# Rotary partners of queries and keys by an exchange of partition halves, with the sine products on GpSimd

## The reference, cut to what matters

```python
def rotate_half(x):
    x1 = x[..., ::2]
    x2 = x[..., 1::2]
    return jnp.stack((-x2, x1), axis=-1).reshape(x.shape)
q, k, v = (proj(Wq, bq), proj(Wk, bk), proj(Wv, bv))
q = q * cos + rotate_half(q) * sin
k = k * cos + rotate_half(k) * sin
attn = jnp.einsum('bhqd,bhkd->bhqk', q, k) * scale
attn = jax.nn.softmax(attn, axis=-1)
```

## Time and profile before

| | |
|---|---|
| median of 3 runs | 600.16 us (597.83 to 601.16) |
| the profiled execution | 598.14 us, span of the core 596.4 us |
| busy share of the span | PE 95%, DVE 83%, ACT 70%, POOL 65% |
| granted TensorE clock, mean | 0.997 |

### The profile page before, as it was taken

One profiled execution on the slowest core, in us unless ns is written; L12 is line 12 of the kernel. 1 busy time (PEld: TensorE's weight loads), 2 busy tenths in 40 slices (PEclk: granted clock), 3 DMA queues, 4 the chain that ended last, 5 costly groups with the idle time before them and its releaser, 6 DMA issues.

```text
span 596.4 us, 19146 instructions
## 1 busy us (share of the span) xinstructions
PE 568.1 (95%) x6702; PEld 438.2 (73%) x6702; DVE 495.8 (83%) x1445; ACT 415.0 (70%) x1038; POOL 385.3 (65%) x817
## 2 busy tenths in 40 slices
PE   8778999999999999999999998999999999999895
PEld 6555666777777777777677786788888888888774
DVE  3679889898988898987788888788888899889763
ACT  1104678778887777788888767767887777777652
POOL 4755556667776667677667776666666677764422
PEclk9989999999999999999999999999999999999999
DMA  7656666566766666745545644335544445441000
GB/s 220 178 157 146 164 155 152 131 151 156 175 152 154 150 150 150 176 117 140 134 117 126 156 128 103 90 90 128 118 119 120 130 128 129 115 121 36 12 20 23
DMA packets 74657, 76.25 MB, mean 128 GB/s; under 512 B 10348, under 2 KB 68908, under 8 KB 70092
## 3 DMA queue, kind: packets, MB, share of 16 engines
q1 hardware_dynamic: 63636, 68.09, 45.0%
q10 hardware_dynamic: 10920, 6.88, 5.5%
HBM read 46.86 MB, written 23.33 MB: 118 GB/s over the span
## 4 chain that ended last, share of the span: by engine, by line
PE 70%; DVE 19%; issue 4%; ACT 3%; POOL 3%; DMA 1%; SPq 0%; ACTq 0%; DVEq 0%; POOLq 0%
PE banks L1630 15%; PE banks L1571 10%; PE banks L1606 9%; PE banks L1472 7%; PE banks L1535 7%; DVE top L1156 5%; DVE top L1155 3%; PE banks L1524 3%; DVE neg_shift L1150 2%; PE banks L1525 2%; PE banks L1504 2%; PE banks L1574 2%; DVE top_sums L1177 1%; DVE top_sums L1180 1%; PE banks L1482 1%
## 5 line engine op out<-in xcount | busy, mean ns | idle before, releaser
L1366 ACT ACTIVATE probs_t<-banks 128x512 f32<-128x512 f32 (+1 forms) x496 | 259.2, 551 | 72.3 <-PE banks L1606 47.8
L1150 DVE TENSOR_REDUCE neg_shift<-banks 128x2 f32<-128x512 f32 x256 | 165.7, 681 | 31.5 <-PE banks L1571 30.0
L1630 PE MATMUL banks<-probs_t,v_ext 128*32 128x256 f32 (+1 forms) x2048 | 116.8, 357 | 0.0
L1571 PE MATMUL banks<-k_stack,q_stack 72*128 72x256 bf16 x512 | 99.7, 276 | 8.0 <-DVE neg_shift L1150 3.3
L1156 DVE MAX8 top<-banks 128x8 f32<-128x256 f32 x256 | 106.1, 414 | 0.0
L1606 PE MATMUL banks<-q_stack,k_stack 75*128 75x256 bf16 x512 | 98.4, 273 | 0.3 <-ACT probs_t L1366 0.2
L1155 DVE MAX8 top<-banks 128x8 f32<-128x128 f32 x256 | 74.1, 290 | 19.8 <-PE banks L1580 19.4
L1026 POOL TENSOR_TENSOR hidden<-up_tanh,gate_half 128x256 f32<-128x256 f32 x93 | 68.3, 736 | 28.6 <-DVE up_tanh L1209 23.5
L1630 PEld LDWEIGHTS banks<-probs_t,v_ext 128*32 128x32 f32 x2048 | 55.4, 109 | 38.8 <-issue 12.8
L1571 PEld LDWEIGHTS banks<-k_stack,q_stack 72*128 72x128 bf16 x512 | 40.4, 98 | 48.1 <-DVE neg_shift L1150 36.4
L1524 PE MATMUL banks<-f_xT_high,w_gate_up 128*128 128x256 f32 x192 | 57.5, 322 | 2.3 <-DVE up_tanh L1209 2.0
(11 more groups left out here) (123 smaller groups left out, 1366.9 us busy)
## 6 DMA issues: line engine op xcount, KB each, us to landing
q_stack<-q_image SPq DMA_DIRECT2D x93, 192.0 KB
k_stack<-k_image SPq DMA_DIRECT2D x93, 192.0 KB
q_image<-qk_parts SPq DMA_DIRECT2D x32, 192.0 KB, 2.4
k_image<-qk_parts SPq DMA_DIRECT2D x32, 192.0 KB, 2.1
q_image<-qk_parts SPq DMA_DIRECT2D x32, 128.0 KB, 2.9
o_image<-out_t SPq DMA_DIRECT2D x32, 128.0 KB, 1.8
out_compact<-o_image SPq DMA_DIRECT2D x32, 64.0 KB
rdenominators<-r_image SPq DMA_DIRECT2D x16, 128.0 KB, 3.5
```

The lines of the kernel that those rows point to most:

```text
L1150: dve.tensor_reduce(m.nm[:, n % STACKS, h, :], scores.rearrange("p (q k) -> p q k", q=TT), AX.X, ALU.max, negate=True).then_inc(reduced, 1)
L1366: act.activation(m.pt[:, (n * Q + g) % GROUPS, i, 0:size], shifted_bank(n, j)[:, 0:size], ACT.Exp if is_soft(n) else ACT.Relu, scale=SCALE ...
L1571: ins = pe.matmul(scores[:, qt * T:(qt + 1) * T], qs[0:STACK, h, qt * P:(qt + 1) * P], ks[0:STACK, h, :], start=True, stop=True)
L1630: ins = pe.matmul(out_bank[32 * i:32 * i + 32, at + skip:at + T], v_windows(v, kt)[:, Q * g + i, :], m.pt[:, (n * Q + g) % GROUPS, i, kt * ...
```

## The change

For items 2 to 15 the second projections go. `project(n, "q")` makes the products of q and k, without partners, into one bank, and `project(n, "k")` falls away. The channels of a head are laid out with the even ones in partitions 0 to 63 and the odd ones in 64 to 127, so that a channel's partner is 64 partitions away. A new `take_raw` on ACT writes both products with their biases to `qk`; `swap_halves` on SP copies its upper half of partitions to the lower half of `rope_sin_terms` and the lower to the upper, in two transfers; `rope_cos_both` on DVE makes the cosine terms; and `split` on POOL waits for the two transfers and multiplies with the sines, in place, ahead of its five instructions. Items 0 and 1 keep the old way. Some places in the order move: `split_q` and `split_k` from -18 and -16 to -17 and -15, stores and loads by one or two steps, `down` from 91 to 93.

```diff
+TURNED_BY_PE = 2
-          split_q=-18, split_k=-16, store_q=-15, store_k=-12, load_q=-12, load_k=-8,
+          split_q=-17, split_k=-15, store_q=-14, store_k=-10, load_q=-11, load_k=-7,
...
+            def swap_halves(n):
+
+                sp.wait_ge(raw_ready, n - TURNED_BY_PE + 1)
+                sp.wait_ge(q_split, n)
+                sp.wait_ge(k_split, n)
+                half = P // 2
+                sp.dma_start(m.ts[0:half, :, :], m.qk[half:P, :, :]).then_inc(swapped, SEM)
+                sp.dma_start(m.ts[half:P, :, :], m.qk[0:half, :, :]).then_inc(swapped, SEM)
...
-                wait_freed(pool, "k" if which and is_soft(n) else "q", n)
+                wait_freed(pool, "k" if which and n < TURNED_BY_PE else "q", n)
+                if is_swapped(n):
+                    pool.wait_ge(swapped, (n - TURNED_BY_PE + 1) * (2 * SEM))
+                    pool.tensor_tensor(m.ts[:, which, :], m.ts[:, which, :], m.cc[:, CC["sin"]:CC["sin"] + T],
+                                       ALU.mult).then_inc(step, 1)
+                    base += 1
+                    pool.wait_ge(step, base)
...
+            def rope_cos_both(n):
+                dve.wait_ge(q_split, n)
+                dve.wait_ge(k_split, n)
+                wait_filled(dve, "q", n)
+                dve.wait_ge(raw_ready, n - TURNED_BY_PE + 1)
+                for which, name in enumerate(("bq", "bk")):
+                    ins = dve.scalar_tensor_tensor(m.tc[:, which, :], bank("q", n)[:, which * T:(which + 1) * T],
+                                                   m.wa[:, WA[name]:WA[name] + 1],
+                                                   m.cc[:, CC["cos"]:CC["cos"] + T], ALU.add, ALU.mult)
+                frees(ins, "q", n)
...
+            def take_raw(n):
+
+                act.wait_ge(q_split, n)
+                act.wait_ge(k_split, n)
+                wait_filled(act, "q", n)
+                for which, name in enumerate(("bq", "bk")):
+                    ins = act.activation(m.qk[:, which, :], bank("q", n)[:, which * T:(which + 1) * T], ACT.Identity,
+                                         bias=m.wa[:, WA[name]:WA[name] + 1], scale=1.0)
+                ins.then_inc(raw_ready, 1)
...
-                names = (use, use + "s") if is_soft(n) else ("q", "k")
+                names = (use, use + "s") if n < TURNED_BY_PE else ("q", "k")
```

More of the change, by code:

```diff
@@ L248, in turn @@
 def turn(n, what):
+    if n == 0 and what in FIRST:
+        return FIRST[what]
     if n == 1 and what in SECOND:
@@ L285, in dense_uses @@
         n = due(step, use)
-        if n is not None and (use != "k" or is_soft(n)):
+        if n is not None and (use != "k" or n < TURNED_BY_PE):
             yield use, n
@@ L295, in q_steps, with is_swapped @@
 def q_steps(n):
-    return 4 * min(n, B) + 3 * max(n - B, 0)
+    return 4 * min(n, TURNED_BY_PE) + 5 * max(min(n, B) - TURNED_BY_PE, 0) + 3 * max(n - B, 0)
+def is_swapped(n):
+    return TURNED_BY_PE <= n < B
 def wait_apart(m, eng, s, value):
@@ L740, in main_phase @@
     rden_loaded = sem("rden_loaded")
+    raw_ready = sem("raw_ready")
+    swapped = sem("swapped")
     ocn_ready = sem("ocn_ready")
@@ L912, in _ @@
                         sp.dma_start(m.ks[r][STACK:SHIFTED, :, :], m.one_rows[:, :]).then_inc(ones_rows, SEM)
+                if (n := due(step, "swap")) is not None and is_swapped(n):
+                    swap_halves(n)
                 if (n := due(step, "load_shift")) is not None:
@@ L1261, in _ @@
                     tau(n)
-                if (n := due(step, "cos_q")) is not None and is_soft(n):
+                if (n := due(step, "cos_q")) is not None and is_swapped(n):
+                    rope_cos_both(n)
+                if (n := due(step, "cos_q")) is not None and n < TURNED_BY_PE:
                     rope_cos(n, 0, "q")
-                if (n := due(step, "sin_q")) is not None and is_soft(n):
+                if (n := due(step, "sin_q")) is not None and n < TURNED_BY_PE:
                     rope_sin(n, 0, "q")
-                if (n := due(step, "cos_k")) is not None and is_soft(n):
+                if (n := due(step, "cos_k")) is not None and n < TURNED_BY_PE:
                     rope_cos(n, 1, "k")
-                if (n := due(step, "sin_k")) is not None and is_soft(n):
+                if (n := due(step, "sin_k")) is not None and n < TURNED_BY_PE:
                     rope_sin(n, 1, "k")
@@ L1424, in _ @@
                     take_qk(n)
+                if (n := due(step, "q")) is not None and is_swapped(n):
+                    take_raw(n)
                 if (n := due(step, "take_v")) is not None:
@@ L1737, in shape_constants @@
     sign = np.where(np.arange(HD) % 2 == 0, f32(-1.0), f32(1.0))[:, None]
-    c[:, CC["cos"]:CC["cos"] + T] = np.repeat(cos, H, axis=0)
-    c[:, CC["sin"]:CC["sin"] + T] = np.repeat(sin * sign, H, axis=0)
+    order = rotary_rows()
+    c[:, CC["cos"]:CC["cos"] + T] = np.repeat(cos[order], H, axis=0)
+    c[:, CC["sin"]:CC["sin"] + T] = np.repeat((sin * sign)[order], H, axis=0)
     q, k = np.arange(P)[:, None], np.arange(P)[None, :]
@@ L1757 @@
     dm = np.arange(D).reshape(H, HD).T.reshape(-1)
-    dms = np.arange(D).reshape(H, HD)[:, np.arange(HD) ^ 1].T.reshape(-1)
+    order = rotary_rows()
+    dmr = np.arange(D).reshape(H, HD)[:, order].T.reshape(-1)
+    dms = np.arange(D).reshape(H, HD)[:, order ^ 1].T.reshape(-1)
     soft_rows = np.arange(D)
```

18 lines of the change are left out of this document (11 added, 7 removed).

## The result

The changed kernel takes 692.9 us (median of 4 runs, 691.1 to 694.8) where the kernel before takes 599.0 (4 runs beside it): a ratio of 1.158, interval 1.154 to 1.162. The direction was forecast; the size was not: 94 us lost, not 30, and outside the range. One run of a kernel of experiment 6 (669.7 us) fell in a slower state of the chip and is left out of that kernel's median and ratio. The page gives a span of 689.1 us for 596.4.

The account below looks back on a forecast made before the run. PE's stream bound the old kernel; the new loop through the exchange would bind. Later rounds 13.0, early rounds 10.1, denominators 5.6 and start-up 1 add 29.7 us to 598.14: 627.8, about 630 as median, range 612 to 652.

Parts of the forecast that it names:

- What is added is a chain: Softmax half: projection, raw tiles, exchange, POOL's splits, `rstd_a`, `norm_a`, transposition, next projection form a loop of 19.2 us against 17.76.
- the three waits: Signs: POOL waits for the exchange 3 to 4 us a round; `norm_a` for `a_norm_bias`, PE for `a_xhat`, 2 us or more.
- The estimate of 0.95: POOL's new product in `split` by the skill's rule: 0.95 us, 28 adding 6 us; the forecast used 0.72 plus 0.07 hand-over.
- PE's 12.2 us don't come off: PE sheds 0.87 us in each of 14 items, 12.2 us, but rounds don't end with PE, so nothing is saved.
- the last sign: PE's busy share in the softmax half should fall below 90%.
- I take 1.9, and 0.1 for POOL: 2.5 us: Exchange on SP: 0.1 wait, 0.4 first issue, 1.9 landing of the second half, 0.1 for POOL, 2.5 us in all.
- charged them to the denominators: ACT's mask copies delay the denominators' copy back, so `normalise` waits 0.7 us in each of eight rounds.
- (3): Exchange lands late, behind the keys' load or with half the partitions reading: 645 us at 3.0, 673 at 5.0; chance 0.14.
- rival (4): PE's clock halves after its idle stand each round, doubling transposition to projection's end: 28 us more, 658 us; chance 0.08.
- The other moved places I cost at nothing: Later `down`, whose residual nobody needs until item 16, and the keys' load, ready well ahead, cost 0 us.
- at 5.6 us in all: `normalise` on POOL waits for the denominators' copy back, 0.7 us in each of eight rounds: 5.6 us.
- the start-up term: Item 2's exchange, ahead of item 1's keys' load on SP, delays that load and PE: 1 us, between bounds 0 and 3.
- one loop of 19.2: Round through exchange and `rstd_a`: POOL 12.59, `norm_a` 0.97, to projection 1.17, to raw tiles 1.99, exchange 2.5 us.

Follow-up runs that it names:

- experiment 6: Changed kernel with the kernel before's places for splits, stores, loads, `down`: 665.3 us; the same plus mask copies moved, `rstd_a` early, exchange issued by ACT: 676.7 us.
- experiment 5: Changed kernel with mask copies moved, `rstd_a` early, `add_bias` one step earlier, `load_k` one later: 661.5 us; variants with denominators' load ahead or ACT's exchange: 656.5 to 687.2.
- experiment 1: Kernel before with only the moved places: 636.2 us; changed kernel without the two exchange transfers, POOL multiplying each channel's own raw value: 640.8 us.
- experiment 3: Changed kernel with mask copies moved from step 13 to step 0 of a round: 672.9 us; changed kernel with ACT issuing the exchange instead of SP: 664.0 us.
- experiment 4: Changed kernel with 24 unread products on PE ahead of its wait for `a_xhat`: 679.2 us; changed kernel with statistics and `rstd_a` six steps earlier: 670.1 us.
- the last version: Changed kernel with old places and statistics, projection and exchange of items 3 to 15 put earlier (643.4 us), that head moved two or three steps earlier again: 640.7 us.

## Why the prediction was wrong, by its own steps

**Right: what is a loop.** The chain named in "What is added is a chain" is in the trace in its order, with the three waits. Its sum in one round of the result, from projection to projection (186.29 to 211.34): POOL 12.54, `norm_a` 0.97, transposition to projection 2.18, projection to raw tiles 2.63, exchange 6.73, together 25.05 us. The first two are as forecast (12.59 and 0.97). The new product takes 0.72, as the row of the sum beside it said. The estimate of 0.95 from the Trainium skill, "GPSIMD Engine Reference", section 4.1 "Engine selection", does not hold for this tile: here the sum of two f32 tiles takes 0.58 us on DVE (L1175, once) and 0.73 on POOL (L998), 1.25 times and not twice. That PE's 12.2 us don't come off was right too, and PE is busy for only 65 to 87% of the 30 us windows from 30 to 360 us, as the last sign had it.

**Wrong, a size: "I take 1.9, and 0.1 for POOL: 2.5 us".** The exchange took 6.73 in this round, 4.2 us more; seven such rounds beside mask copies make about 30 us. The row used was a store of `out_t` with little ahead of it; the shortest landings were 2.3 to 2.9. The mask copies were in view: the prediction charged them to the denominators, from the same row, and not to the exchange that is issued beside them. The rival that had a late exchange was (3), with 0.14. It looked for the keys' load or for the two halves as the reason, and not for the mask copies; with the keys' load right ahead it landed in 4.8 to 5.8 (experiment 5), and whether reading half of the partitions matters no run shows. With the exchange absent 52 us go (experiment 1), with the copies moved 20 (experiment 3). The Trainium skill, "DMA: Bandwidth & Descriptors", section "Issuing engines are not separate DMA queues", says that transfers of all issuing engines run on the same 16 DMA engines and interleave. The trace agrees: 6.0 us beside ACT's copies, with a DMA share of 0.83 to 0.95 between 190 and 193 us.

**Wrong, a size: the clock, rival (4), against which stood "here a round is still more than 80% full".** A stand of 3.04 us was followed by half clock, with PE inside the loop just then: 1.0 us more on the way to the projection, 0.6 on the way to the raw tiles. Idle products gave 14 us back, with the clock only in part restored (experiment 4). It was forecast at 28 if it came, and given 0.08; in the event it came together with (3).

**Wrong, a term put at nothing: "The other moved places I cost at nothing".** They lose 37 us alone and 28 in the changed kernel. `down` two steps later was said to be read by a residual that nobody needs until item 16. Nobody needs the residual's result, but its read frees a dense bank, and the v projection needs the bank: 13 us. The stores and loads were looked at for when their data is ready, not for what is queued behind them on SP: 40 us of standing, behind which the denominators wait. The prediction had the way of the denominators only from their copy back on, at 5.6 us in all. In one round of the result (127.3 to 149.1) the chain doesn't pass the exchange at all but q's image, landing in 4.21 us, k's image, in 3.20, `r_image`, in 4.65, and only then the copy back, in 4.56.

**Wrong: the start-up term, 1 us.** The prediction has the exchange of item 2 ahead of the keys' load of item 1 on SP. It stands behind it: that load is issued at 29.79 (30.31 before) and the exchange at 32.80, and PE stands 2.56 us for the load instead of 2.39. Its size is 0.2 us at most; the reading of the order was wrong.

**Wrong: that one loop is the round.** The sum took one loop of 19.2 and no other. The traces show at least three of 20 to 25 us: through `rstd_a`; through SP's stores, loads and denominators; and, at the old places, through `split_shift` and PE's wait for it. Parts give back 20 to 29 us alone and 36 together. In part that is because each opens only one loop, and in part because two of them put something new into the way, the keys' load ahead of the exchange and DVE's statistics ahead of the split.

**How far the 94 us are shown.** Exchange 52 by leaving it out, which includes the copies beside it and part of the half clock (mean clock 0.957 without it, 0.926 with); the other 42 remain without it, where the places alone cost 37. But the parts do not simply add: with the old places 66 us are lost, which with the 37 of the places alone would make 103. No run leaves out the exchange at the old places, so what ACT's raw tiles, POOL's added products and the shared buffers cost by themselves is not shown. What holds the last version at 641 is not settled: it has waits for the shared `qk` buffer, for ACT and for DVE, and early rounds (40 to 120 us) at a clock of 0.67 to 0.84, but no kernel isolated one of these.

## What to carry to other kernels

A transfer put into a loop between engines has to be priced with what the other queues issue in the same microseconds, not by the quietest row of its size, and issued several steps ahead of its reader: here seven steps of lead in place of two took the wait for it from 82.3 us to 4.4, where a faster landing only shortened it. A place moved in an in-order queue is a change of its own: ask for each what is queued behind it and which bank or buffer its last reader frees. And where a round has several loops of nearly one length, the gain from opening one is bounded by the next, so list them all before a sum is made of one. Work that is moved ahead of another in an in-order engine brings its own wait with it: with `rstd_a` early POOL stood 66 and 82 us for it in two kernels.

## What the runs showed that was not expected

A 64x512 f32 copy between partition halves, the second of two, landed 2.3 to 2.9 us after its issue in four rounds, 6.0 to 6.7 in seven beside two copies from another queue of 424 KB together, and 4.8 to 5.8 right behind 576 KB from its own queue. PE's busy time rose by 31 us with less work: the first scores of a head (L1624, L1571 before) took 302 ns in the mean instead of 276, and in the 30 us windows from 30 to 360 us the clock was 0.77 to 0.90, where it had been 0.94 to 1.00. From 185 to 187 us, at clock 0.50, PE is busy for 1.00 of each microsecond, so a busy share alone reads as a bound that isn't there.
